# A two-layer decoder on one core: a third key block earlier, an output projection per tile, and copies moved to the head of a step

## The chip, the core and the metric

The kernel runs on one core of one Trainium2 chip. The metric is the time of one execution in device microseconds. TensorE does the matrix products (and transposes, as products with the identity), VectorE and ScalarE the elementwise work, GpSimd small operations and gathers, SyncE issues DMAs. The engines run their own instruction streams in program order and meet at semaphores.

## The reference

The input is eight sequences of 256 rows with 512 numbers each, and a context of the same shape. Two layers of three blocks each run over it, every block as a residual on a layer norm:

```
x = x + _L0_attn_ref(_layernorm(x, axis=-1), ...)     # 16 heads, rotary, causal window of 64
x = x + _L0_xattn_ref(_layernorm(x, axis=-1), ctx, mask, ...)   # 16 heads over the context
x = x + _L0_ffn_ref(_layernorm(x, axis=-1), ...)      # 64 experts, 6 per row, and a shared one
x = x + _L1_attn_ref(_layernorm(x, axis=-1), ...)     # state-space mixer in chunks
x = x + _L1_xattn_ref(_layernorm(x, axis=-1), ctx, ctx, gamma)  # 8 heads, attends over features
x = x + _L1_ffn_ref(_layernorm(x, axis=-1), ...)      # 8 low-rank experts on a dense layer
```

The change touches the parts that compute these lines. In the cross attention of layer 0 the context gives keys and values, and the result is divided by the sums of the exponentials:

```
k = _nan_clean(proj(at, Wk, bk, T))
probs = jax.nn.softmax(scores, axis=-1)
ctx = jnp.einsum('bhst,bhtd->bhsd', probs, v)
```

In layer 1 the mixer ends with `yn @ out_proj_w.T`, where yn are rows normalized per head; the attention after it computes `sm = softmax(q k * scale)` and `gamma * (sm v)` over 512 context features.

## The kernel before

The program has five stages, one after the other: phase 1 (both attentions of layer 0, function `phase1`), the shared expert with the router, the 64 experts, the mixers (function `mixers`, which holds the mixer and the attention of layer 1), and the feed-forward block of layer 1. In every stage each engine has its own function with an order written out by hand; `wait_ge` on a semaphore is the only thing that joins them. PSUM has eight banks, and `bank(n)` is one of them, 512 numbers on each of 128 partitions. Rows are handled in two tiles of 128 (NT = 2), the 512 columns in four blocks (KC = 4).

Phase 1 loops over the eight sequences. In the cross attention of sequence i the engines already begin with sequence i + 1: TensorE multiplies the keys of the next context, block by block (`keys`, through line 188), and ScalarE copies each block with its bias out of PSUM (`keys_copy`, line 615). Blocks 0 and 1 go to bank 7, blocks 2 and 3 to banks 2 and 3. At the end of the cross attention TensorE turns the next sequence's normalized rows (`rows_to_cols`, line 182), into banks 2 and 3 as well. VectorE takes the reciprocal of the sums of all heads (line 1102), TensorE spreads it over the 32 rows of each head with four products (line 934, into banks 0 and 1), ScalarE copies the two halves (line 710), VectorE multiplies them with the attention's result (line 1107), and TensorE applies the output projection (line 188 with `w_xo`). Between the spreads and the projection stand key blocks 2 and 3.

The mixers take the sequences in four pairs (`first`, `second`). At the end of a pair's mixer TensorE turns the gated rows of a sequence tile by tile (`turn_gated`, line 2404), ScalarE copies the two turned tiles (`gated_copy`, line 2212), and TensorE projects each tile (`project_out`, line 2473 through 188). The wait ahead of the projection of tile j asks for both copied tiles:

```
pe.wait_ge(sy["colsT_ready"], 8 * (s // 2) + 4 + NT * (b + 1))
```

Then comes the pair's attention, a loop of 32 steps (PAIRS = 16 for each sequence, HP = 32) with some steps behind. In step i TensorE makes the scores of two heads (line 2487), VectorE their minima (line 2756), ScalarE two exponentials (line 2310); two steps later TensorE turns the probabilities (line 2497), ScalarE and VectorE copy one half each (lines 2318 and 2763), and every second step TensorE multiplies them with the context (`returned`, line 2518). Each sequence has two groups of 16 heads. When a group's sums are complete, VectorE takes their reciprocals, TensorE turns them (`turn_recips`, line 2530, in steps 10, 17, 26 and 33), and ScalarE copies them to the tile `y` (`copy_recips`, line 2301, in steps 11, 18, 27 and 34). The turned reciprocals of group 0 lie in bank 7 and those of group 1 in bank 6; the products of the groups are collected in these banks too, so that `returned` waits for the copies before it begins a new group. In ScalarE's step the order was: exponentials of step i, turned copy of step i - 1, other work, copy of the reciprocals.

Of the kernel before, what the change touches and what calls it, by code (L numbers as in the profile page):

```python
# [40 lines left out]
NT = S // P  # L41
KC = D // P
# [291 lines left out]
def phase1(nc, sy, const, dr, held, nseq=NSEQ):  # L334
# [6 lines left out]
    with ExitStack() as ctx:  # L341
# [83 lines left out]
        def turned_in(i):  # L425
            return NT * 2 * i
# [2 lines left out]
            return NT * (2 * i + 1)  # L429

        def key_bank(i, c):
            return bank(7 if i >= 1 and c < 2 else 2 + c % 2)

        def turned_bank(at, j):
            return bank(2 + j if at and at % (2 * NT) == 0 else j)
# [157 lines left out]
        def _(act):  # L593
# [66 lines left out]
            for i in range(nseq):  # L660
                for c in range(2 * KC):
                    act.wait_ge(sy["qk_proj"], due("qk_proj", i, c + 1))
                    act.activation(qk_raw[:, c, :], bank(2 + c % 2)[:, 0:S], ACT.Copy,
                                   scale=-QK_SCALE if c < KC else 1.0).then_inc(sy["qk_raw_ready"], 1)
                    if i == 0:
                        split_hi(K if c < KC else V, c % KC)
                values_copy(i, 0)
                for n in range(LPAIRS):
                    c, r = n // 2, 2 * (n % 2)
                    act.wait_ge(sy["lmin_ready"], due("lmin_ready", i, n + 1))  # L670
                    if n >= 3:
                        act.wait_ge(sy["probsT_psum"], due("probsT_psum", i, n - 2))
                    for k in range(2):
                        scores = bank_pair(2 * (n % 2))[:, k, :]
                        act.activation(probs[:, n % 3, k, 0:P], scores[:, 0:P], ACT.Exp, bias=smin[:, n, k, 0:1],
                                       scale=-1.0, accum_out=ssum[:, c, 0, r + k:r + k + 1])
                        act.activation(probs[:, n % 3, k, P:S], scores[:, P:S], ACT.Exp,
                                       bias=smin[:, n, k, 1:2], scale=-1.0,
                                       accum_out=ssum[:, c, 1, r + k:r + k + 1]).then_inc(sy["probs_ready"], 1)
                    if n == 1:  # L680
                        values_copy(i, 1)
                    if i == 0 and 2 <= n < 2 + KC:
                        split_hi(XQ, n - 2)
                    if n in (5, 7):
                        copy_recips(i, (n - 5) // 2)
                copy_recips(i, 2)
                copy_recips(i, 3)
                if i == 0:
                    act.wait_ge(sy["w1b_in"], n_late * 16)
                    keys_copy(0, 0, KC)  # L690
                cols_copy(turned_attn(i))
                for c in range(KC):
                    act.wait_ge(sy["xq_psum"], due("xq_psum", i, c + 1))
                    act.activation(qk[:, c, :], bank(6 + c % 2)[:, 0:S], ACT.Identity, bias=bq[:, c:c + 1]
                                   ).then_inc(sy["xq_ready"], 1)
                for n in range(LPAIRS):
                    act.wait_ge(sy["clipped_ready"], due("clipped_ready", i, 2 * n + 2))
                    act.activation(xprobs[:, n % 4], xprobs[:, n % 4], ACT.Exp, scale=1.0 / ROOT_HD
                                   ).then_inc(sy["xprobs_ready"], 1)
                    if i < last and n in (0, LPAIRS - 1):  # L700
                        keys_copy(i + 1, n // (LPAIRS - 1), n // (LPAIRS - 1) + 1)
                    if i == last:
                        shared_opening(n)
                if i < last:
                    cols_copy(turned_in(i + 1))
                else:
                    shared_chunks_hi(2, 4)
                for half in range(2):
                    act.wait_ge(sy["xrecT_psum"], due("xrecT_psum", i, half + 1))
                    act.activation((cosq, sinq)[half][:].rearrange("p c s -> p (c s)"), bank(half)[:, :], ACT.Copy  # L710
                                   ).then_inc(sy["xrec_copied"], 1)
                if i < last:
                    keys_copy(i + 1, 2, KC)
                else:
                    shared_chunks_hi(4, len(MS_CHUNKS))
            sy.end_turn(act, 0, 0)
# [2 lines left out]
        def _(pe):  # L719
# [24 lines left out]
            def keys(i, chunks):  # L744

                for c in chunks:
                    if i == 0 and c >= 2:
                        pe.wait_ge(sy["xk_ready"], due("xk_ready", i, c - 1))
                    if i >= 1 and c == 1:
                        pe.wait_ge(sy["xk_ready"], due("xk_ready", i, 1))  # L750
                    if i >= 1 and c >= 2:
                        pe.wait_ge(sy["colsT_lo"], turned_in(i) + NT)
                    project_pe(pe, key_bank(i, c)[:, 0:S], lambda kc: w_x["k"][:, kc, c * P:(c + 1) * P],
                               lambda kc: ctxT[:, kc, :]).then_inc(sy["xk_psum"], 1)
# [118 lines left out]
            for i in range(nseq):  # L873
# [53 lines left out]
                pe.wait_ge(sy["clipped_ready"], due("clipped_ready", i, 2 * LPAIRS))  # L927
                if i < last:
                    rows_to_cols(hn, normed_in(i + 1), turned_in(i + 1))
                else:  # L930
                    shared_gate_up(0, 0)
                pe.wait_ge(sy["xrec_ready"], due("xrec_ready", i, 1))
# [3 lines left out]
                    if c % 2:  # L936
                        ins.then_inc(sy["xrecT_psum"], 1)
                if i < last:
                    keys(i + 1, range(2, KC))
                else:  # L940
                    shared_gate_up(0, 1)
                pe.wait_ge(sy["xattn_ready"], due("xattn_ready", i, 2))
# [1006 lines left out]
def mixers(nc, sy, const, dr, tiles, rows, router_raw, opening, nseq=NSEQ):  # L1949
# [3 lines left out]
    with ExitStack() as ctx:  # L1953
# [245 lines left out]
        def _(act):  # L2199
# [133 lines left out]
            for p in range(npair):  # L2333
# [33 lines left out]
                    high(first, j)  # L2367
                q0 = HP * p
                for i in range(HP + 3):
                    if i < HP:  # L2370
                        exponentials(q0 + i)
                    if p + 1 == npair and i == HP:
                        for j in range(NT):
                            ffn_rows_hi(j)
                    if 1 <= i <= HP:
                        turned_copy(q0 + i - 1)
                    if p + 1 == npair and i == 13:
                        ffn_fixed_hi()
                    if i in (8, 9):
                        high(second, i - 8)  # L2380
                    if i in (11, PAIRS + 11):
                        copy_recips(first + i // PAIRS, 0)
                    if i in (PAIRS + 2, HP + 2):
                        copy_recips(first + i // PAIRS - 1, 1)
                    if p + 1 < npair and i in (HP + 1, HP + 2):
                        rows_copy(first + 2 + i - HP - 1)
            act.wait_ge(sy["f_router"], 1)
# [4 lines left out]
        def _(pe):  # L2392
# [76 lines left out]

            def project_out(s, j):  # L2470
                b = s % 2
                pe.wait_ge(sy["colsT_ready"], 8 * (s // 2) + 4 + NT * (b + 1))
                project_pe(pe, bank(2 + 4 * b + j), lambda kc: hT[b][:, kc, j * P:(j + 1) * P],
                           lambda kc: w_mo[:, kc, :]).then_inc(sy["out_psum"], 1)

# [1025 lines left out]
```

## Time and profile before

| | us |
|---|---|
| median of 3 runs | 3139.12 (3132.17 to 3144.71) |
| profiled execution | 3157.93 |
| its span from first to last instruction | 3156.0 |
| TensorE busy | 2980.2 (94%) |
| VectorE busy | 2302.3 (73%) |
| ScalarE busy | 1579.9 (50%) |
| GpSimd busy | 809.4 (26%) |
| mean granted clock of TensorE | 0.98 |

The busy shares are means over stages with different limits; matrix products are pipelined and their ends are modelled. The granted clock is given as a share of full speed.

### The profile page before, as it was taken

What the parts mean: (1) busy time and instruction counts of PE and PEld (TensorE: products, weight loads), DVE (VectorE), ACT (ScalarE), POOL (GpSimd) and SP (SyncE); (2) the same over time, 40 slices, a digit from 0 to 9 for tenths busy, and PEclk for the clock granted to TensorE, in tenths of its full rate; (3) what the DMA queues carried; (4) which work ended last, traced back from release to release, by engine and by line L of the source; (5) the groups of instructions that cost most, each with busy time, mean ns of one, the idle gap of its engine ahead of it and who ended that gap; (6) DMA issues with size and microseconds to landing.
All of it is one profiled execution on the core that took longest, in us unless ns stands there. A gap on an engine that the chain in (4) does not pass through costs nothing. (4 is left out here: it accounts for less than half of the span.)

```text
span 3156.0 us, 61772 instructions
## 1 busy us (share of the span) xinstructions
PE 2980.2 (94%) x23073; PEld 2400.3 (76%) x23073; DVE 2302.3 (73%) x4321; ACT 1579.9 (50%) x3643; POOL 809.4 (26%) x974
## 2 busy tenths in 40 slices
PE   7999999998999999999999969999999989999999
PEld 5666666665998888888888846767666678888888
DVE  5665666665875788888888668878786877777776
ACT  3323333334221455555555436666666765555554
POOL 1221122121664111111111073341503022222222
PEclk9999999999999999999999979999999999999999
DMA  6325333321311677777777642121210042222222
GB/s 277 123 82 190 120 137 111 124 100 39 117 49 37 227 249 237 250 237 252 235 253 236 235 141 64 62 78 45 78 42 12 13 141 75 77 76 76 76 75 71
DMA packets 146539, 403.96 MB, mean 128 GB/s; under 512 B 39488, under 2 KB 48192, under 8 KB 133520
## 3 DMA queue, kind: packets, MB, share of 16 engines
q1 hardware_dynamic: 107888, 325.36, 30.0%
q0 software_dynamic: 18976, 50.45, 5.6%
q10 hardware_dynamic: 19456, 25.18, 2.3%
q8 instruction: 143, 2.34, 0.3%
q14 instruction: 76, 0.62, 0.1%
HBM read 344.06 MB, written 54.76 MB: 126 GB/s over the span
## 5 line engine op out<-in xcount | busy, mean ns | idle before, releaser
L288 POOL DMA_INDIRECT hr<-normed_rows,idx x128 | 123.3, 964 | 635.3 <-PE psum L302 592.6
L3016 POOL TENSOR_TENSOR mixf<-act 128x256 f32<-128x256 f32 x128 | 143.1, 1118 | 458.7 <-DVE act L3282 458.7
L174 POOL TENSOR_SCALAR ve<-mv 128x1 f32<-128x1 f32 x112 | 36.0, 321 | 791.4 <-DVE mv L965 523.0
L328 PE MATMUL psum<-xT_hi,wgu_hi 128*128 128x192 f32 (+1 forms) x1536 | 227.8, 270 | 1.4 <-PEq L1125 0.8
L328 PE MATMUL psum<-xT_hi,wgu_lo 128*128 128x192 f32 (+1 forms) x1536 | 223.1, 267 | 0.0
L328 PE MATMUL psum<-xT_lo,wgu_hi 128*128 128x192 f32 (+1 forms) x1536 | 222.6, 267 | 0.0
L1742 ACT ACTIVATE eth<-psum 128x192 f32<-128x192 f32 (+1 forms) x192 | 63.2, 330 | 299.1 <-PE psum L328 292.5
L328 PEld LDWEIGHTS psum<-xT_hi,wgu_hi 128*128 128x128 f32 (+1 forms) x1536 | 189.8, 182 | 26.6 <-ACT wgu_hi L1726 21.5
L2310 ACT ACTIVATE scratch<-psum,smin 128x512 f32<-128x512 f32 x256 | 173.7, 686 | 61.3 <-DVE smin L2756 59.1
L328 PEld LDWEIGHTS psum<-xT_hi,wgu_lo 128*128 128x128 f32 (+1 forms) x1536 | 190.3, 182 | 0.0
L328 PEld LDWEIGHTS psum<-xT_lo,wgu_hi 128*128 128x128 f32 (+1 forms) x1536 | 190.2, 182 | 0.0
L2756 DVE TENSOR_REDUCE smin<-psum 128x2 f32<-128x1024 f32 x128 | 155.4, 1217 | 37.2 <-PE psum L2487 36.5
L3282 DVE TENSOR_TENSOR act<-act,maskT 128x512 f32<-128x512 f32 x128 | 88.1, 689 | 116.9 <-ACT act L3058 116.4
L2497 PEld LDWEIGHTS psum<-ident,scratch 128*128 128x128 f32 x1024 | 110.6, 142 | 57.8 <-issue 38.9
L2497 PE MATMUL psum<-ident,scratch 128*128 128x128 f32 x1024 | 146.6, 283 | 6.1 <-DVE scratch L2763 2.9
L1852 DVE SCALAR_TENSOR_TENSOR eact<-eth,psum 128x192 f32<-128x192 f32 (+1 forms) x192 | 67.5, 352 | 111.9 <-ACT eth L1742 109.5
L3292 DVE TENSOR_TENSOR ca_lo<-act,ca_hi 128x512 fp32r<-128x512 f32 x128 | 134.2, 1049 | 12.4
L729 PE MATMUL psum<-hT_hi,w_slot 128*128 128x256 f32 x768 | 110.9, 289 | 11.9 <-ACT hT_hi L607 5.9
L1265 POOL DMA_INDIRECT slot_token<-tok_i,slot_w x96 | 104.6, 1090 | 67.5 <-DVE slot_r L1590 39.1
L2124 POOL DMA_INDIRECT yk<-expert_out,slots x84 | 86.1, 1025 | 122.9 <-issue 48.2
L1096 DVE TENSOR_SCALAR arena<-psum,hi 128x512 f32<-128x512 f32 x128 | 87.5, 745 | 40.7 <-PE psum L835 40.6
L3071 ACT ACTIVATE ca_hi<-act 128x512 fp32r<-128x512 f32 x128 | 81.0, 633 | 66.4 <-DVE act L3282 66.4
(466 smaller groups left out, 8681.9 us busy)
## 6 DMA issues: line engine op xcount, KB each, us to landing
w_sg<-in_w_gu_dram SPq DMA_DIRECT2D x32, 1408.0 KB
w_su<-in_w_gu_dram SPq DMA_DIRECT2D x32, 1408.0 KB
w_slot<-w_split SPq DMA_DIRECT2D x21, 2048.0 KB, 13.3
w_raw<-in_w_dram SPq DMA_DIRECT2D x128, 256.0 KB, 2.6
w_sd<-in_w_d_dram SPq DMA_DIRECT2D x32, 512.0 KB
wd<-in_w_d_dram SPq DMA_DIRECT2D x32, 512.0 KB
expert_out<-so ACTq DMA_DIRECT2D x64, 256.0 KB, 5.3
w_slot<-w_split SPq DMA_DIRECT2D x28, 512.0 KB, 5.1
```

The lines of the kernel that those rows point to most:

```text
L288: pool.indirect_dma_start(out=xg[0:w, t, :], out_offset=None, in_=rows, in_offset=bass.IndirectOffsetOnAxis(ap=idx[0:w, t:t + 1], axis=0)) ...
L328: ins = pe.matmul(bank(2 + m)[0:w, gu * CAP:(gu + 1) * CAP], wgu2[wp][:, gu, kc, m0:m0 + w], xT2[xp][:, kc, :], start=(i == 0 and kc == 0) ...
L729: ins = pe.matmul(out, lhs_of(lp, kc), rhs_of(rp, kc), start=(m == 0 and kc == 0), stop=(m == 2 and kc == KC - 1))
L1096: dve.tensor_scalar(xprobs[:, n % 4, kt], bank_pair(2 * (n % 2))[:, :, kt * S:(kt + 1) * S], hi[:, kt:kt + 1], -SCORE_CLIP * ROOT_HD, ALU. ...
L1265: pool.indirect_dma_start(out=dr["slot_token"], out_offset=bass.IndirectOffsetOnAxis(ap=slot_w[s % 2][:, j, k:k + 1], axis=0), in_=tok_i[s ...
L2124: pool.indirect_dma_start(out=gathered(s, NT * k + j), out_offset=None, in_=dr["expert_out"], in_offset=bass.IndirectOffsetOnAxis(ap=slots ...
L2310: act.activation(prob[:, q % 4, k, :], bank_pair(2 * (q % 2))[:, k, :], ACT.Exp, bias=smin[b][:, n, k:k + 1], scale=-1.0, accum_out=ssum[b ...
L2497: ins = pe.transpose(bank(4 + k)[:, mc * P:(mc + 1) * P], prob[:, q % 4, k, mc * P:(mc + 1) * P], ident)
L2756: dve.tensor_reduce(smin[(q // PAIRS) % 2][:, q % PAIRS, :], bank_pair(2 * (q % 2)), AX.X, ALU.min).then_inc(sy["smin_ready"], 1)
L3016: pool.tensor_tensor(mixf[:, g % LAG, :], act2[:, g % LAG, 0, :], act2[:, g % LAG, 1, :], ALU.add).then_inc(sy["f_mix"], 1)
L3282: dve.tensor_tensor(act2[:, g % LAG], act2[:, g % LAG], maskT[(g // FC) % 2][:, 2:4, :], ALU.mult).then_inc(sy["f_ca"], 1)
L3292: dve.tensor_tensor(ca2[1][:, g % LAG], act2[:, g % LAG], ca2[0][:, g % LAG].bitcast(F32), ALU.subtract).then_inc(sy["f_ca_lo"], 1)
```

## The change

In phase 1 key block 2 of the next sequence goes to bank 7, like blocks 0 and 1, and waits for the copy of block 1. TensorE multiplies it after the turned rows and ahead of the spreads; ScalarE copies it ahead of the two copies of the spread reciprocals. In the mixers the projection of tile j waits for the turned tiles up to j alone, and the copy of the turned reciprocals stands first in ScalarE's step.

```diff
         def key_bank(i, c):
-            return bank(7 if i >= 1 and c < 2 else 2 + c % 2)
+            return bank(7 if i >= 1 and c < 3 else 2 + c % 2)
...
                 if i < last:
                     cols_copy(turned_in(i + 1))
+                    keys_copy(i + 1, 2, 3)
                 else:
                     shared_chunks_hi(2, 4)
...
                 if i < last:
-                    keys_copy(i + 1, 2, KC)
+                    keys_copy(i + 1, 3, KC)
...
-                    if i >= 1 and c == 1:
-                        pe.wait_ge(sy["xk_ready"], due("xk_ready", i, 1))
-                    if i >= 1 and c >= 2:
+                    if i >= 1 and c in (1, 2):
+                        pe.wait_ge(sy["xk_ready"], due("xk_ready", i, c))
+                    if i >= 1 and c == 3:
                         pe.wait_ge(sy["colsT_lo"], turned_in(i) + NT)
...
                 if i < last:
                     rows_to_cols(hn, normed_in(i + 1), turned_in(i + 1))
+                    keys(i + 1, (2,))
...
                 if i < last:
-                    keys(i + 1, range(2, KC))
+                    keys(i + 1, (3,))
...
                 for i in range(HP + 3):
+                    if i in (11, PAIRS + 11):
+                        copy_recips(first + i // PAIRS, 0)
+                    if i in (PAIRS + 2, HP + 2):
+                        copy_recips(first + i // PAIRS - 1, 1)
                     if i < HP:
                         exponentials(q0 + i)
...
                     if i in (8, 9):
                         high(second, i - 8)
-                    if i in (11, PAIRS + 11):
-                        copy_recips(first + i // PAIRS, 0)
-                    if i in (PAIRS + 2, HP + 2):
-                        copy_recips(first + i // PAIRS - 1, 1)
...
             def project_out(s, j):
                 b = s % 2
-                pe.wait_ge(sy["colsT_ready"], 8 * (s // 2) + 4 + NT * (b + 1))
+                pe.wait_ge(sy["colsT_ready"], 8 * (s // 2) + 4 + NT * b + j + 1)
```

## Rows read from the trace of the kernel before

**Rows 1.** The page's first part: busy us (share of the span) xinstructions.

```profile
PE 2980.2 (94%) x23073; PEld 2400.3 (76%) x23073; DVE 2302.3 (73%) x4321; ACT 1579.9 (50%) x3643; POOL 809.4 (26%) x974
```

**Rows 2.** TensorE's waits, whole span: us in total, times, longest us.

```profile
PE psum L2518 <- ACT y L2301: 7.0, 6, 1.5
PE psum L188 <- ACT hT L2212: 6.8, 8, 1.1
...
PE psum L934 <- DVE recb L1102: 6.3, 8, 0.9
...
PE psum L2518 <- DVE scratch L2763: 3.2, 3, 1.4
```

**Rows 3.** Timeline, second transition: start, length, engine, line, operation [idle before <-releaser].

```profile
200.66 0.47 ACT L615 ACTIVATE xkT<-psum,bk 128x256 f32<-128x256 f32 x1 [0.99 <-PE psum L188]
...
202.55 1.76 DVE L1102 RECIPROCAL recb<-psum 128x256 f32<-128x256 f32 x1 [3.98 <-PE psum L853]
...
204.37 1.99 PE L934 MATMUL psum<-recb,spread 128*128 128x256 f32 x8 [0.86 <-DVE recb L1102]
205.53 0.60 ACT L710 ACTIVATE cosq<-psum 128x512 f32<-128x512 f32 x1 [1.34 <-PE psum L934]
...
206.20 3.62 PE L188 MATMUL psum<-ctxT,w_xk 128*128 128x256 f32 x16
...
207.03 0.69 DVE L1107 TENSOR_TENSOR oT<-psum,sinq 128x512 f32<-128x512 f32 x1 [0.17 <-ACT sinq L710]
...
209.65 7.03 PE L188 MATMUL psum<-w_xo,oT 128*128 128x512 f32 x16
```

**Rows 4.** Timeline around the second pair's projection of its second sequence.

```profile
2091.86 0.69 ACT L2290 ACTIVATE y<-y,grstd 128x128 f32<-128x128 f32 x2 [1.11 <-POOL grstd L2152]
...
2093.41 1.06 ACT L2212 ACTIVATE hT<-psum 128x512 f32<-128x512 f32 x2
...
2094.52 3.70 PE L188 MATMUL psum<-w_mo,hT 128*128 128x512 f32 x8 [1.11 <-ACT hT L2212]
...
2096.62 1.47 DVE L2750 SCALAR_TENSOR_TENSOR h_lo<-h,h_hi 128x512 fp32r<-128x512 f32 x2
```

**Rows 5.** Timeline, attention of the second pair, steps 10 to 13.

```profile
2124.25 0.66 PE L2530 MATMUL psum<-ident,y 128*128 128x128 f32 x4
...
2126.42 0.60 ACT L2318 ACTIVATE scratch<-psum 128x512 f32<-128x512 f32 x1 [0.35 <-PE psum L2497]
...
2128.91 0.69 ACT L2301 ACTIVATE y<-psum,small 128x512 f32<-128x512 f32 x1
...
2129.86 1.08 PE L2518 MATMUL psum<-scratch,cxT 128*32 128x128 f32 x32 [1.13 <-ACT y L2301]
...
2131.88 1.23 DVE L2756 TENSOR_REDUCE smin<-psum 128x2 f32<-128x1024 f32 x1 [1.65 <-PE psum L2487]
2132.46 0.60 ACT L2318 ACTIVATE scratch<-psum 128x512 f32<-128x512 f32 x1 [1.51 <-PE psum L2497]
```

**Rows 6.** Timeline, same attention, its second sequence, steps 27 to 29.

```profile
2172.39 0.69 ACT L2301 ACTIVATE y<-psum,small 128x512 f32<-128x512 f32 x1
...
2173.34 1.08 PE L2518 MATMUL psum<-scratch,cxT 128*32 128x128 f32 x32 [1.37 <-DVE scratch L2763]
...
2175.36 1.23 DVE L2756 TENSOR_REDUCE smin<-psum 128x2 f32<-128x1024 f32 x1 [1.22 <-PE psum L2487]
```

**Rows 7.** Two stretches between products: us, busy by engine, PEclk, DMA, GB/s.

```profile
2001.84:2010.65 8.81, 8.81 (x60) 6.27 (x60) 5.95 (x11) 3.98 (x10) 1.15 (x4) 0.50 0.01 2
2173.34:2178.18 4.84, 4.84 (x60) 3.49 (x60) 3.55 (x6) 3.24 (x10) 0.79 (x2) 1.00 0.00 0
```

**Rows 8.** Stretches from spread to spread in phase 1, and their sum.

```profile
204.37:295.34 90.97, 86.13 (x713) 58.92 (x713) 57.66 (x100) 32.58 (x100) 18.09 (x25) 1.00 0.46 173
...
572.76:670.20 97.44, 91.90 (x712) 62.71 (x712) 57.96 (x100) 32.79 (x100) 18.10 (x25) 0.93 0.31 111
...
sum 651.12, PE 613.68 PEld 419.11 DVE 402.72 ACT 232.70 POOL 127.00; mean PE 87.67 PEld 59.87 DVE 57.53 ACT 33.24 POOL 18.14
```

## The prediction

> **What bounds the kernel now.** I read the page's busy shares first: TensorE is busy for 94% of the span [rows 1], so the time is the length of its instruction stream plus its waits. The second view is the list of TensorE's waits. Three of its lines stand on places that the change touches [rows 2]: the spread matmuls wait for the reciprocal on VectorE (6.3 us in 8 waits), the mixers' output projection for the turned rows that ScalarE copies (6.8 us in 8), and the products of the second attention (L2518) for the copied reciprocals (7.0 us in 6). A fourth line, L2518 on VectorE's copy, 3.2 us in 3, belongs to the third partly; I come back to it. The third view is the timeline around one case of each, to see whether the other engines stand still at the same time. Only if they do is a removed wait given back as time.
>
> **Part one, key block 2 ahead of the spreads (seven transitions between sequences).** Before, TensorE turns the next rows, waits 0.86 us for the 1.76 us reciprocal, runs the eight spread records, then sixteen records of key blocks 2 and 3, and then the output projection [rows 3]. The waits add to 6.3 over eight; the last sequence has no next keys and is not changed, and seven times 0.86 is 6.0. Nothing is added or removed: eight matmul records, and on ScalarE one copy of 0.47 us, come earlier. From start to start the sixteen records take 209.65 - 206.20 = 3.45 us, so one block is 1.73. It fits into the wait and sticks out by 1.73 - 0.86 = 0.87 at most, so that the spreads run 0.8 to 0.9 later than now, counted from the turned rows.
>
> What is late next is the chain spread, ScalarE copy, VectorE product, for which the projection waits. Now the second product ends at 207.03 + 0.69 = 207.72 and the projection starts at 209.65, 1.93 later, covered by both key blocks [rows 3]. Afterwards the chain ends 0.8 to 0.9 later (208.5 to 208.6) while the projection wants to start 0.86 earlier (208.8). About 0.2 us of cover is left. The moved ScalarE copy (0.47) has its block ready when the spreads start, and the first spread copy comes 1.16 after their start, behind 1.34 of ScalarE idle; the moved copy lies in that. The new wait of block 2, for the copy of block 1 in the same bank, is long met: that kind of copy ends at 200.66 + 0.47 = 201.13, over 2 us before the turned rows are done at 204.37 - 0.86 = 203.51. Behind the waiting block would stand the spreads and all that follows. Bounds per transition: 0.86 gained, or, if the cover of 0.2 is overrun by the whole moved copy, 0.86 - 0.5. I take 0.86, seven times: **6.0 us**. No DMA moves; those of SyncE that follow (weights of the next sequence) wait for TensorE's own products and move along.
>
> The ends of TensorE's rows deserve care. By starts alone, the projection would move up by the spreads' first record too, a little more than the gap. The Trainium skill (Perfetto Trace Analysis, section Tensor Engine Instruction) says that TensorE's end times are computed and not observed; a sum from starts would be up to about 0.94 per transition, 6.6 us in place of 6.0. The trace agrees that ends overlap: the spreads' row ends at 204.37 + 1.99 = 206.36 and the next begins at 206.20 [rows 3].
>
> **Part two, the output projection per turned tile (four pairs of sequences).** The eight waits are of two kinds: four of 1.1 (second sequence of a pair), which leaves 6.8 - 4.4 = 2.4, or 0.6 each, for the first. In the second, ScalarE copies two tiles in 1.06 from 2093.41, and TensorE starts 0.05 after the second, with 1.11 of waiting [rows 4]. With a wait per tile it starts after the first: 1.06 / 2 = 0.5 earlier. The scores behind it need the low part of the normalized rows, whose first tile is there by about 2096.62 + 0.73 = 2097.4, while the projection, 3.70 long, ends near 2097.7 even then. So 0.5 is kept; four pairs give **2.0 us**. In the first sequence the same 0.5 is gained at the projection but not kept: the next thing on TensorE is the turning of the second sequence, which needs ScalarE's scaled rows, done at 2091.86 + 0.69 = 2092.55 after a wait for GpSimd [rows 4], and that chain is not driven by TensorE. The copies at 2093.41 follow from there as now, so I take 0. Bounds for the part: 0 and 6.8.
>
> **Part three, the copies of the turned reciprocals at the head of ScalarE's step.** Sixteen copies, of which four (the last of each pair) come in a step that has nothing ahead of them; twelve move in front of two exponentials and a turned copy. Of these the eight with group 0 hold TensorE up. In one loop [rows 5]: the reciprocals are turned by 2124.25 + 0.66 = 2124.91. ScalarE reaches the head of the step at 2126.42 + 0.60 = 2127.02 but copies only at 2128.91, and L2518 starts at 2129.86 after 1.13 of waiting. From 2127.02 the copy would be done at 2127.7, before TensorE gets there at 2128.73: the wait goes whole. Do the others follow? The next minima on VectorE had stood idle for 1.65 and ScalarE's next turned copy for 1.51, both behind TensorE [rows 5]; both hold more than 1.13. The price on ScalarE is that two exponentials come up to 0.69 later, the copy's length, but the exponentials after them come at the same time as now, since the copy has only changed places, and the 1.51 of idle lie right behind. What is next in line afterwards is VectorE with 0.5 to spare.
>
> In the second sequence of two pairs the same wait is put down to VectorE's copy, 1.37 [rows 6]. There L2518 starts 0.26 after the end of the ScalarE copy (2172.39 + 0.69 = 2173.08), exactly as in rows 5 (2129.60 to 2129.86). It is the same wait, named wrongly. VectorE's idle time behind it is 1.22, so 1.22 is what can be gained. The sum: 7.0 for the six and 2 x 1.22 = 2.4, **9.4 us**. The four copies of group 1 in the eighteenth step delay nobody that I can see, and I count them as 0; their bounds are 4 x 0.69 = 2.8 lost and, should a loop wait unseen, as much gained.
>
> Here a rule speaks against the change. The row shows ScalarE with the copy behind work that was ready later. The Trainium skill (TensorE: Matmul & The Clock Gate, section Architectural detail: the array is 16× 32×32, not 1× 128×128) says that ScalarE works its queue strictly in order; so a copy at the head whose reciprocals are not yet turned holds all exponentials of the step. By the rule alone each lateness would be paid in full; by the rows the reciprocals are ready 2.1 us ahead of the head (2124.91 to 2127.02), and it costs nothing. The trace agrees with the order that the rule states.
>
> **The clock.** In the first pair's second sequence TensorE fell to half of its 2.4 GHz right at the 1.5 us wait for the copy; the stretch between two products took 8.81 at 0.50 against 4.84 at 1.00 in the next pair [rows 7]. If the fall goes with its wait, 4.0 more are won. I count half, 2.0, since falls also come where no wait of this size goes.
>
> **The sum.** 6.0 + 2.0 + 9.4 + 2.0 = 19.4 us. The profiled execution took 3157.9, so 3138.5 for its like. The runs shown have a median of 3139.1, 18.8 below it, and I take that distance as unchanged: **3119.7, rounded 3120 us**.
>
> **Rivals.**
> - The cover at the projection of phase 1 is overrun. For it: 0.2 us is little, and the moved copy of 0.47 stands ahead of the spread copies. Against: ScalarE idles there. It takes 0.5 x 7 = 3.5 back: 3123.2.
> - ScalarE becomes the end of the attention loop: twelve late pairs of exponentials cost 12 x 0.69 = 8.3. For it: in the steps before, ScalarE runs nearly without gaps. Against: its 1.51 idle behind each copy [rows 5]. 3128.0.
> - The copy does not release the product: L2518 waits in truth for the turned probabilities that ScalarE copies just ahead of the reciprocals. Then 9.4 stay: 3129.1. Against it speaks the program: that product needs turned copies only up to the one of 2126.42.
> - Slower: the clock. In phase 1 a sequence takes 90.97 at a granted clock of 1.00 and 97.44 at 0.93; the seven together take 651.1 [rows 8], 14.3 above seven of the fast ones. A shorter sequence meets the clock's decisions in another phase. If all seven ran as the slow one, they would take 682.1, 31.0 more; less the gain of the other terms (17.4) that is 13.6 slower: 3152.7. It decides from 17.4 / 6.5, some three further sequences. For it: the falls differ between sequences of the same work. Against: the change takes idle time out of TensorE and puts none in.
>
> **Chances.** Forecast 0.66, the cover 0.10, ScalarE 0.11, the product's other wait 0.07, the clock 0.06. What a measurement can tell from no change is about 0.5%, 15.7 us: faster means below 3123.4, slower above 3154.8. The forecast is over the bound with 0.55 of its 0.66 (without the clock's 2.0 it stands at 3121.7, only 1.7 below the bound), the first rival with half; together 0.60 faster. Half of the clock's case goes beyond the bound upward, 0.03. The rest, 0.37, is the same. The range: at the low end the whole of the 4.0 and half of the 14.3 go with the waits, 3119.7 - 2.0 - 7.2 = 3110; at the high end it takes in the second and third rival, 3131. The forecast's own range is 3113 to 3125.
>
> **What would show it.** Right: no wait before the spreads but key records there; about 90.1 between the spreads of two sequences at clock 1.00; the wait at L188 for the copied tile down to 0.5 in the second sequences and near 0 in the first; L2518 without a wait on the copied reciprocals in all eight loops, and VectorE's idle of 1.65 down to about 0.5. Wrong: a new wait of the projection on VectorE's product in phase 1; exponentials that make the scores or the turning wait; more stretches at half clock.

## Result and profile after

The changed kernel takes 3114.27 us in the median of 5 runs (3109.52 to 3115.61), the kernel before 3138.83 in the median of 5 beside them: ratio 0.9921, interval [0.9907, 0.9934], 24.6 us faster. Set against the kernel before once more on another chip (run e9_whole below) it took 3113.98 against 3134.10: ratio 0.9931 [0.9916, 0.9946], 20.1 us. The forecast was 3120, in a range of 3110 to 3131. The profiled execution after took 3110.33, its span is 3108.5, its mean granted clock 0.988 (before: span 3156.0, clock 0.980). Of the runs below one, of e1_keys, took 9496.98 us, three times the others, and is left out of that kernel's median.

The two profiled executions differ by 47.6 us, nearly twice what the medians differ by, so they can't be subtracted as wholes. Most of the surplus lies ahead of the mixers. Their first projection starts at 1912.35 in the profile before, but at 1894.85 and 1895.60 in two experiments that leave all work ahead of it as before (e2_project, e3_copies). About 17 us belong to that one execution, near the 18.8 by which it lies over the median. Below, stretches are compared place by place.

The page's line of busy times after, which answers to [rows 1]; TensorE's busy time counts its slow stretches at their length:

```profile
PE 2954.8 (95%) x23073; PEld 2384.2 (77%) x23073; DVE 2301.0 (74%) x4321; ACT 1579.0 (51%) x3643; POOL 808.7 (26%) x974
```

The counts are the same; VectorE, ScalarE and GpSimd are busy as long as before, within 1.3 us. TensorE's waits after (us in total, times, longest), the lines that answer to [rows 2]:

```profile
PE psum L2489 <- ACT scratch L2312: 2.8, 9, 0.3
...
PE psum L188 <- ACT hT L2214: 2.5, 4, 0.6
...
PE psum L2406 <- ACT y L2292: 1.3, 4, 0.5
...
PE psum L2520 <- DVE scratch L2765: 0.4, 1, 0.4
PE psum L936 <- DVE recb L1104: 0.3, 1, 0.3
```

The spreads now wait in the last sequence alone, which has no next keys. The projection's wait is down from 6.8 in 8 to 2.5 in 4. The product (L2518 before, L2520 now) has no line on the copied reciprocals any more, and the one on VectorE's copy fell from 3.2 to 0.4. Some waits have grown a little: the scores wait 2.8 us in 9 for exponentials (L2489; before, as L2487, 2.5 in 8), and the turning of the gated rows waits 1.3 in 4 for ScalarE's scaled rows (L2406; before, as L2404, 0.4 in 1). The timeline of the second transition, beside [rows 3]; its first row is of the kernel before, the others are of the kernel after:

```profile
202.42 1.09 PE L182 MATMUL psum<-ident,hn 128*128 128x128 f32 x8
```

```profile
201.90 1.09 PE L182 MATMUL psum<-ident,hn 128*128 128x128 f32 x8
202.03 1.76 DVE L1104 RECIPROCAL recb<-psum 128x256 f32<-128x256 f32 x1 [3.98 <-PE psum L854]
...
202.82 1.89 PE L188 MATMUL psum<-ctxT,w_xk 128*128 128x256 f32 x8
...
204.55 1.89 PE L936 MATMUL psum<-recb,spread 128*128 128x256 f32 x8
204.75 0.47 ACT L615 ACTIVATE xkT<-psum,bk 128x256 f32<-128x256 f32 x1 [1.08 <-PE psum L188]
205.62 0.60 ACT L711 ACTIVATE cosq<-psum 128x512 f32<-128x512 f32 x1 [0.39 <-PE psum L936]
...
206.28 1.89 PE L188 MATMUL psum<-ctxT,w_xk 128*128 128x256 f32 x8
...
207.11 0.69 DVE L1109 TENSOR_TENSOR oT<-psum,sinq 128x512 f32<-128x512 f32 x1 [0.17 <-ACT sinq L711]
...
208.01 3.17 PE L188 MATMUL psum<-w_xo,oT 128*128 128x512 f32 x7
```

The reciprocal ends at 203.79, under the key block, and the spreads start without a wait. From the start of the turned rows to that of the projection it is 208.01 - 201.90 = 6.11; before, it was 209.65 - 202.42 = 7.23. The second product ends at 207.80, 0.21 ahead of the projection: that is all the cover that is left.

The second pair's projection of its second sequence, beside [rows 4], waits 0.63 in place of 1.11 and starts behind the first of the two tiles of the copy at 2056.19. What it gains the scores keep, for the low part follows 2.09 after its start, as before (2.10):

```profile
2054.64 0.70 ACT L2292 ACTIVATE y<-y,grstd 128x128 f32<-128x128 f32 x2 [1.11 <-POOL grstd L2154]
...
2056.19 1.06 ACT L2214 ACTIVATE hT<-psum 128x512 f32<-128x512 f32 x2
...
2056.82 3.70 PE L188 MATMUL psum<-w_mo,hT 128*128 128x512 f32 x8 [0.63 <-ACT hT L2214]
...
2058.91 1.47 DVE L2752 SCALAR_TENSOR_TENSOR h_lo<-h,h_hi 128x512 fp32r<-128x512 f32 x2
```

The same pair's attention, steps 10 to 13 of the first sequence and 27 to 28 of the second, beside [rows 5, 6]:

```profile
2086.56 0.66 PE L2532 MATMUL psum<-ident,y 128*128 128x128 f32 x4
...
2088.73 0.60 ACT L2320 ACTIVATE scratch<-psum 128x512 f32<-128x512 f32 x1 [0.36 <-PE psum L2499]
...
2089.22 0.68 ACT L2303 ACTIVATE y<-psum,small 128x512 f32<-128x512 f32 x1
...
2090.98 1.08 PE L2520 MATMUL psum<-scratch,cxT 128*32 128x128 f32 x32
...
2093.00 1.23 DVE L2758 TENSOR_REDUCE smin<-psum 128x2 f32<-128x1024 f32 x1 [0.45 <-PE psum L2489]
2093.58 0.60 ACT L2320 ACTIVATE scratch<-psum 128x512 f32<-128x512 f32 x1 [0.51 <-PE psum L2499]
...
2131.31 0.69 ACT L2303 ACTIVATE y<-psum,small 128x512 f32<-128x512 f32 x1
...
2133.01 1.08 PE L2520 MATMUL psum<-scratch,cxT 128*32 128x128 f32 x32
```

The reciprocals are turned by 2087.22, the head of the step comes at 2089.22, the copy is done at 2089.90, and the product starts 1.08 later without a wait. VectorE's idle time behind it fell from 1.65 to 0.45, ScalarE's from 1.51 to 0.51. Counted from the pair's first projection, in us of the profiled executions (a product is counted at its start, the last one at the start of its last record):

| place | before | after |
|---|---|---|
| product of step 12, pairs 2 and 3 | 44.49, 44.50 | 43.32, 43.32 |
| product of step 28, pairs 2 and 3 | 87.97, 87.97 | 85.35, 85.33 |
| last product, pairs 2, 3 and 4 | 102.64, 102.64, 101.09 | 100.12, 100.12, 98.62 |

Two windows of after from the product of step 28 to the next (us, busy by engine, granted clock, DMA share, GB/s), in the first and the second pair, beside [rows 7]: the first pair's is at full clock now, 5.37 in place of 8.81.

```profile
1969.88:1975.25 5.37, 5.14 (x62) 3.54 (x61) 5.30 (x10) 3.86 (x11) 0.79 (x2) 1.00 0.00 2
2133.01:2137.84 4.83, 4.83 (x62) 3.48 (x61) 4.76 (x8) 4.32 (x13) 0.79 (x2) 1.00 0.01 2
```

And the second and the last stretch from spread to spread, beside [rows 8]: the second is 1.14 shorter than before at the same clock of 1.00, and stretches are still longer where the clock falls.

```profile
204.55:294.38 89.83, 85.88 (x713) 59.00 (x712) 57.63 (x100) 32.58 (x100) 18.03 (x25) 1.00 0.47 175
655.18:748.03 92.85, 85.71 (x702) 57.21 (x700) 55.69 (x96) 36.81 (x108) 18.72 (x23) 0.96 0.19 66
```

### The profile page after: what moved, and what is told of

The parts are those of the page before. It is cut to its first block and busy times, and to the rows that moved or that the text cites. A ratio compares the mean times of both kernels' runs of the same rounds, so it can differ in the third digit from the quotient of the medians.

```text
span 3108.5 us, 61772 instructions
## 1 busy us (share of the span) xinstructions
PE 2954.8 (95%) x23073; PEld 2384.2 (77%) x23073; DVE 2301.0 (74%) x4321; ACT 1579.0 (51%) x3643; POOL 808.7 (26%) x974
```

## Experiments

The theory is that of the prediction: three separate waits, each given back as time. The first four kernels take the change apart; the next four put a strain on what the theory says is hidden. "Before" is the median of the kernel before on the same chip: 3137.45 for the first four, 3135.17 for the next four, 3134.10 for the last two.

**e1_keys: the key block alone.** The whole change without its two edits in the mixers:

```diff
-   pe.wait_ge(sy["colsT_ready"], 8 * (s // 2) + 4 + NT * b + j + 1)
+   pe.wait_ge(sy["colsT_ready"], 8 * (s // 2) + 4 + NT * (b + 1))
...   (both groups' copy_recips back behind high(second, i - 8))
```

> The key block alone: key block 2 ahead of the spreads, everything else as before. Theory (the removed waits are worth their start-to-start length): from spread to spread 89.8 us at full clock in place of 90.97, that is 1.13 us in each of seven transitions, 7.9 us together, so about 3131 against 3138.8; the mixers' waits stay (L188 on the copied tile 1.1 us, L2518 on the copied reciprocals 1.1 us). Rival A (the gap of 0.86 in the profile is the whole gain): 90.1 and 6.0 us. Rival B (the gain of the whole change came from the clock): a time anywhere in 3130 to 3140 with 89.8, and fewer stretches at half clock.

Measured: 3128.2 in the median of six runs, 9.3 under the kernel before, ratio 0.9965 [0.9953, 0.9977]. From spread to spread, here the second stretch:

```profile
204.19:294.03 89.84, 85.86 (x714) 58.84 (x713) 57.64 (x100) 32.61 (x100) 18.09 (x25) 1.00 0.47 175
```

That is 90.97 - 89.84 = 1.13 per transition, and seven of them 7.9 us. So rival A is out: the gap of 0.86 in [rows 3] was too small a measure.

**e2_project: the projection per turned tile alone.**

```diff
-   pe.wait_ge(sy["colsT_ready"], 8 * (s // 2) + 4 + NT * (b + 1))
+   pe.wait_ge(sy["colsT_ready"], 8 * (s // 2) + 4 + NT * b + j + 1)
```

> The output projection per turned tile alone. Theory: in each of four pairs TensorE's wait for the second copied tile goes (0.6 us in the first sequence, about 0.5 of 1.1 in the second); in the first it is taken back by the turning of the second sequence, so 0.5 us a pair are kept, 2 us together: 3136 to 3137 against 3138.8. Rival (both are kept): 1.0 us a pair, 4 us, 3134 to 3135.

Measured: 3135.34, 2.1 under, ratio 0.9994 [0.9983, 1.0006]. The interval holds 1, so the time alone shows nothing. The profile does: the wait is 2.5 in 4, as in the whole change, the turning of the gated rows waits 1.3 in 4 in place of 0.4 in 1, which is where the first sequences' gain goes, and from the second pair's first projection to the third's it is 166.54, against 167.00 in e1_keys, whose mixers are those of before. That is 0.46 per pair, and four pairs give 1.8.

**e3_copies: the copies at the head alone.**

```diff
     for i in range(HP + 3):
+        if i in (11, PAIRS + 11):
+            copy_recips(first + i // PAIRS, 0)
+        if i in (PAIRS + 2, HP + 2):
+            copy_recips(first + i // PAIRS - 1, 1)
         if i < HP:
             exponentials(q0 + i)
...
         if i in (8, 9):
             high(second, i - 8)
-        if i in (11, PAIRS + 11):
...
```

> The copies of the turned reciprocals at the head of ScalarE's step alone (both groups). Theory: all eight waits of L2518 for the copied reciprocals go and the pair's attention is 2.4 to 2.7 us shorter, 10.4 us together without the clock; 3126 to 3129. Rival (ScalarE becomes the end of the loop): the waits go but the attention is less than 1 us shorter in each pair, 3135 to 3139.

Measured: 3126.81, 10.6 under, ratio 0.9965 [0.9948, 0.9983]. The last products of pairs 2 to 4 come at 100.12, 100.13 and 98.61 from the first projection, as in the whole change; from pair to pair it is 164.50 against 167.00. ScalarE does not become the end of the loop. In its list of waits the product's line has gone, those of the other two parts have stayed:

```profile
PE psum L188 <- ACT hT L2212: 6.8, 8, 1.1
PE psum L934 <- DVE recb L1102: 6.3, 8, 0.9
...
PE psum L2518 <- DVE scratch L2763: 0.4, 1, 0.4
```

The line on VectorE's copy (3.2 before) went to 0.4 by moving a ScalarE copy alone: it was the same wait, put down to the other engine.

**e4_group0: the whole change, with group 1's copies at their old place.**

```diff
     for i in range(HP + 3):
         if i in (11, PAIRS + 11):
             copy_recips(first + i // PAIRS, 0)
-        if i in (PAIRS + 2, HP + 2):
-            copy_recips(first + i // PAIRS - 1, 1)
...
+        if i in (PAIRS + 2, HP + 2):
+            copy_recips(first + i // PAIRS - 1, 1)
         if p + 1 < npair and i in (HP + 1, HP + 2):
```

> The whole change, but with the copy of group 1 (steps 18 and 34) at its old place in ScalarE's step. Theory (the copies of group 1 delay nobody): the same as the whole change within 1 us, 3113 to 3116, and the attention of a pair as long as there within 0.2 us. Rival (they cost or give up to their length, 0.69 in each of four loops): 2.8 us more or less than the whole change, and the stretch from the product of step 12 to that of step 20 longer or shorter by 0.5 to 0.7.

Measured: 3112.89, ratio 0.9917 [0.9899, 0.9934], and in the third pair the last product at 100.13, as with group 1 moved (100.12). Group 1's move is worth nothing that the runs show, either way.

**e5_both_blocks: key block 3 ahead of the spreads as well.** This takes away the last cover of the chain spread, ScalarE, VectorE.

```diff
-   return bank(7 if i >= 1 and c < 3 else 2 + c % 2)
+   return bank(7 if i >= 1 else 2 + c % 2)
...
-   keys(i + 1, (2,))
+   keys(i + 1, (2, 3))
...   (block 3 waits for block 2's copy; its own copy goes ahead of the spread copies)
```

> The whole change, and key block 3 ahead of the spreads too (in bank 7, behind the copy of block 2). Theory (what is left between spreads and projection must cover the chain spread, ScalarE copy, VectorE product, and only 0.2 us of cover is left in the whole change): the spreads come 1.7 us plus a wait of 0.6 to 0.8 for the bank later, and the projection then waits about 1.5 to 1.9 us for VectorE's second product, so a transition is 2.1 to 2.4 us longer than in the whole change, 15 to 17 us together: 3129 to 3131. Rival (the chain is no bound, TensorE's stream alone is): 0.6 to 0.8 us a transition for the bank's wait, 5 us: 3119.

Measured: 3129.81, ratio 0.9985 [0.9976, 0.9995], 15.5 above the whole change by medians of two chips. Spread to spread takes 92.37, 2.54 more than after. This agrees with the theory and not with the rival. The first line is from the list of waits, the others from the timeline of the second transition:

```profile
PE psum L188 <- DVE oT L1103: 9.9, 7, 1.4
```

```profile
204.89 1.89 PE L188 MATMUL psum<-ctxT,w_xk 128*128 128x256 f32 x8
207.35 1.99 PE L188 MATMUL psum<-ctxT,w_xk 128*128 128x256 f32 x8 [0.56 <-ACT xkT L615]
209.18 1.89 PE L932 MATMUL psum<-recb,spread 128*128 128x256 f32 x8
...
211.74 0.69 DVE L1103 TENSOR_TENSOR oT<-psum,sinq 128x512 f32<-128x512 f32 x1 [0.17 <-ACT sinq L711]
212.48 2.84 PE L188 MATMUL psum<-w_xo,oT 128*128 128x512 f32 x6 [1.41 <-DVE oT L1103]
```

The projection waits 1.41 in all seven transitions, until 0.05 after the second product ends (212.43). Block 3 waits besides for the copy of block 2 in the one bank, 0.56 here. Counted from start to start, against 1.73 for such a row without a wait, the two are 212.48 - 209.18 - 1.73 = 1.57 and 207.35 - 204.89 - 1.73 = 0.73, and block 3's own row, behind the wait, takes 0.10 more: 2.40 of the 2.54. So a block behind the spreads is needed, and with one the cover just suffices.

**e6_context_later: the whole change, and the copy of the second sequence's turned context behind that of its gated rows.** It aims at the 0.6 that is left of the projection's wait.

```diff
-    context_high(second)
     gated_copy(second)
+    context_high(second)
```

> The whole change, and ScalarE's copy of the next context's high part (1.04 us) behind the copies of the second sequence's turned rows instead of ahead of them. Theory (in the second sequence ScalarE's context copy, not TensorE, holds the turned rows up): the wait at L188 in the second sequences goes from 0.6 to 0.5 or less and the copies start 0.4 to 0.5 us earlier, worth 0.4 us in each of four pairs, 1.6 us: 3112 to 3113. Rival (the low parts of the normalized rows are late next): 0, and the scores behind the projection wait for VectorE.

Measured: 3112.32, ratio 0.9927 [0.9910, 0.9944]. The projection's waits are down to 1.0 in 4. The second sequence's projection starts 8.77 after the first's in place of 9.16, and the 0.39 is kept to the last product (99.72 against 100.12, counted from the first projection in the second pair).

**e7_between: the copies between exponentials and turned copy.**

```diff
     for i in range(HP + 3):
+        if i < HP:
+            exponentials(q0 + i)
         if i in (11, PAIRS + 11):
...
-        if i < HP:
-            exponentials(q0 + i)
```

> The whole change, but with the copies of the turned reciprocals between the step's exponentials and its turned copy. Theory (the product L2518 is released by this copy alone): the copy ends 0.6 us earlier than before the change and 1.4 later than at the head, so L2518 waits 0.4 to 0.7 us in all eight loops and the time is 3 to 5 us above the whole change, 3117 to 3120. Rival 1 (the turned copy releases it): L2518 waits 1.1 or more again, 3123 or more. Rival 2 (ScalarE is the end of the loop): no wait, and the time of the whole change.

Measured: 3121.90, ratio 0.9948 [0.9931, 0.9966], 7.6 above the whole change and above the range of the theory. The six runs go from 3109.80 to 3123.37: two, with a mean clock of 0.988 and 0.989, lie at 3114.97 and 3109.80, as low as the whole change, and four, with 0.985, at 3121.47 or more. So the time alone separates the two kernels poorly, and the profile has to. The waits have one line again; then the second pair's timeline at step 11, and the window of the first pair's step 28:

```profile
PE psum L2520 <- ACT y L2303: 5.8, 8, 1.0
```

```profile
2096.52 0.69 ACT L2303 ACTIVATE y<-psum,small 128x512 f32<-128x512 f32 x1
...
2097.45 1.08 PE L2520 MATMUL psum<-scratch,cxT 128*32 128x128 f32 x32 [0.63 <-ACT y L2303]
```

```profile
1971.61:1980.42 8.81, 8.81 (x61) 6.27 (x61) 6.44 (x11) 4.21 (x11) 1.15 (x4) 0.50 0.01 2
```

The product starts 0.24 after the copy's end (0.26 in [rows 5]), and step 12's comes 0.72 later than in the whole change, 0.45 earlier than before. The last products are 1.59, 1.55 and 1.37 later in pairs 2 to 4. It is the two exponentials ahead of the copy that cost, more than the turned copy: 0.72 of the 1.17 that the whole move gains at step 12. The first pair has its half-clock stretch again, 8.81 at 0.50, as before; the theory had left that out.

**e8_step_earlier: group 0's copies at the head of the step before.** Here the copy meets reciprocals that aren't turned yet.

```diff
-        if i in (11, PAIRS + 11):
+        if i in (10, PAIRS + 10):
             copy_recips(first + i // PAIRS, 0)
```

> The whole change, but with the copies of group 0 at the head of the step before (10 and 26), ahead of the turning of the reciprocals on TensorE. Theory (ScalarE takes its queue in order, and the margin of about 2 us at the head of step 11 is what makes the copy free): the copy waits 0.5 to 1 us at the head of step 10 for TensorE's turned reciprocals and the exponentials of step 10 start about 1.1 us later; the loop has some 0.4 us of slack there, so 0.3 to 0.8 us are lost in each of eight loops, 3117 to 3121. Rival (the wait is hidden, since the exponentials wait for VectorE's minima anyway): the time of the whole change.

Measured: 3115.33, ratio 0.9941 [0.9923, 0.9959], below the theory's range and within 1.4 of both medians of the whole change, so the time alone shows no loss. The second pair's timeline, step 10 of its first sequence:

```profile
2090.27 0.65 PE L2532 MATMUL psum<-ident,y 128*128 128x128 f32 x4
...
2090.96 0.69 ACT L2303 ACTIVATE y<-psum,small 128x512 f32<-128x512 f32 x1 [0.49 <-PE psum L2532]
...
2091.55 0.68 ACT L2312 ACTIVATE scratch<-psum,smin 128x512 f32<-128x512 f32 x1
...
2093.13 0.49 PE L2489 MATMUL psum<-cx_hi,h_hi 32*128 32x512 f32 x2 [0.28 <-ACT scratch L2312]
```

ScalarE waits 0.49 at the copy with the exponentials behind it, and TensorE's scores then wait 0.28 for the exponentials. The rule that spoke against the change, ScalarE's strict order in the Trainium skill (TensorE: Matmul & The Clock Gate, section Architectural detail: the array is 16× 32×32, not 1× 128×128), agrees with the row. Step 12's product comes 0.33 later than in the whole change, the last of the pair 0.57; over the four pairs it is 2.2, the low end of what was expected. So the place has a floor: one step earlier the copy pays for its order in the queue, and at the head of step 11 it doesn't.

**e9_whole and e10_later_again: the whole change and e6_context_later side by side.** The edits are those shown.

> The whole change, unaltered, once more on the chip of the next run, for a direct comparison with it. Theory (the parts add): 3112 to 3117 us. If the earlier 24.6 us held several us of luck with the clock, it comes nearer to the sum of the parts alone, 20.9 us under the kernel before.

> The whole change with the copy of the turned context of the second sequence behind that of its gated rows. Theory: the 0.39 us that the profile showed in each of four pairs is kept, so 1.6 us under the whole change in the run beside it. Rival: it is given back later in the pair, and the two are equal within 0.5 us.

Measured: 3113.98, ratio 0.9931 [0.9916, 0.9946], and 3112.23, ratio 0.9928 [0.9913, 0.9943]. The second is 1.75 under the first by medians, but their runs overlap (3110.61 to 3115.41, 3108.41 to 3114.57). By the profile the later context copy brings the second projection 0.38 to 0.39 forward in pairs 2 to 4, in both of its executions, and 0.37 to 0.41 of it is there at the product after step 28's. It has the lowest median of the kernels, by a difference that the profile shows and the times alone can't.

## Why the prediction was right

**The key block: right in kind, its size too small (6.0 forecast, 7.9 measured).** The step that failed is "the waits add to 6.3 over eight ... seven times 0.86". From start to start the transition was 1.95 (turned rows to spreads), 1.83 (spreads), 3.45 (two blocks), 7.23 in all. Now it is 0.92 (turned rows), 1.73 (block 2), 1.73 (spreads) and 1.73 (block 3), 6.11. So the wait was 1.95 - 0.92 = 1.03 by starts, for the row ahead of it is drawn with an end that reaches into the gap: that row is 1.09 long, yet the next starts 0.92 after it where nothing waits. The Trainium skill (Perfetto Trace Analysis, section Tensor Engine Instruction) says that such ends are computed, and the two rows agree. Another 0.10 is the spreads' slower first record, which went with the wait. The estimate from starts in the prediction (0.94, which no row shows) pointed the right way and was passed over; it still lacked most of the overlap. The cover at the projection is the forecast 0.2 (0.21) by luck, for its terms were off and cancel: the spreads run 0.70 later and not 0.87 (2.65 after the turned rows in place of 1.95), the chain behind them is 0.10 shorter, and the projection comes 1.12 earlier and not 0.86. The first rival did not come; e5_both_blocks shows that it looked at the right place, for there the projection waits once its cover is gone.

**The projection: right (2.0 forecast).** The second sequences' waits fell from 1.1 to 0.6, and the first sequences' 0.6 went from the list. The pair got 0.46 shorter, once, not twice (e2_project), as the chain over GpSimd in [rows 4] said: the first sequence's gain stands as a wait at the next turning (L2406, 1.3 in 4). The time of that part alone lies within what can be told from no change.

**The copies: right, a little small (9.4 forecast, 10.3 measured).** Pairs 2 to 4 end 2.52, 2.52 and 2.47 earlier; in the first pair the product of step 12 comes 1.17 earlier from the scores, and step 28's 1.62 earlier from the eighth, 2.79 together. The step that was small is the 1.22 for the second sequences of pairs 2 and 3, which was VectorE's idle time: TensorE's own wait was 1.37 [rows 6], and from the product of step 20 to that of step 28 it gained 22.63 - 21.19 = 1.44, of which the last steps give back 0.1. The rest is again that a printed wait is a little too small: 1.13 in step 12 of the second pair gave 1.17, and the fourth pair's waits of 1.11 and 1.12 gave 2.47. The third rival, that the product waits for the turned probabilities, is wrong: with the copy ahead of them the wait is gone (e3_copies), with it between exponentials and probabilities over half of it stays (e7_between, 5.8 in 8). The second, that ScalarE becomes the end, is wrong: its idle time of 1.51 took up the late exponentials, and 0.51 is left. The sign of it that the prediction named, exponentials that make the scores wait, is there only in small: the scores wait 2.8 us in place of 2.5, and the turning of the probabilities 6.9 in place of 5.4 for the two copies of turned halves (3.9 and 3.0, before 2.9 and 2.5); some 0.1 of the gain is gone by the pair's last product.

**The clock at the first pair: right at its place, the gain not shown (2.0 of 4.0 forecast).** The stretch at step 28 is 8.81 at half clock in the kernel before, in e1_keys and in e7_between and 8.38 (at 0.53) in e2_project, the four profiles in which the product waits there. It is 5.37 in all eight profiles without the wait. So 3.4 was to be had at this place, not 4.0: the first pair needs 5.37 at full clock where the second needs 4.84. But mostly the half clock only moves. The stretch from that product to the next pair's first projection, in e1_keys, in the profile after and in e9_whole, the same kernel once more:

```profile
1975.06:2057.16 82.10, 79.20 (x515) 62.60 (x515) 61.63 (x134) 47.54 (x130) 43.62 (x58) 0.92 0.26 78
```

```profile
1969.88:2047.66 77.78, 74.10 (x515) 58.51 (x515) 61.86 (x134) 47.55 (x132) 43.71 (x58) 1.00 0.28 83
```

```profile
1967.56:2049.75 82.19, 78.41 (x515) 62.44 (x514) 60.94 (x134) 47.52 (x132) 43.63 (x58) 0.94 0.26 78
```

With the wait the four profiles take 80.32 to 83.53. Without it three (after, e5_both_blocks, e10_later_again) take 77.75 to 77.81 at a clock of 1.00, and five (e3_copies, e4_group0, e6_context_later, e8_step_earlier, e9_whole) 81.08 to 82.21 at 0.94 to 0.96, as long as with it (0.5 of such a difference is the projection's, where a kernel has that edit). So the step "If the fall goes with its wait, 4.0 more are won" failed: the fall left its place in eight of eight, and the time was won in three of eight. On the mean the eight are 1.6 shorter than the four, less than the scatter within either group, so the 2.0 of the sum is neither shown nor refuted.

**The clock in phase 1.** The slower rival, more falls in phase 1, did not come; there were fewer. The seven stretches from spread to spread take 647.78 to 651.12 in the three profiles with the old phase 1 (before, e2_project, e3_copies) and 633.30 to 636.54 in the eight with one key block moved. The nearest two are e3_copies and e1_keys:

```profile
sum 647.78, PE 610.82 PEld 416.97 DVE 402.51 ACT 232.81 POOL 127.28; mean PE 87.26 PEld 59.57 DVE 57.50 ACT 33.26 POOL 18.18
```

```profile
sum 636.54, PE 605.46 PEld 413.68 DVE 401.58 ACT 232.81 POOL 127.27; mean PE 86.49 PEld 59.10 DVE 57.37 ACT 33.26 POOL 18.18
```

They differ by 11.2, more than the 7.9 of the keys. Of the seven stretches five or six lie below a clock of 1.00 in the three profiles, and two to four in the eight. So with the moved block falls are rarer here, in eight profiles against three, which the prediction's sum had at nothing and only the low end of its range allowed for. What of it stays to the end is open: e1_keys is 9.3 faster by its runs, and their mean clock over the whole execution (0.983 to 0.985) is that of the kernel before (0.980 to 0.986).

**The sum.** By places it is 7.9 + 1.8 + 10.3 = 20.0, and the clock comes on top in some executions. The parts alone, by medians, give 9.3 + 2.1 + 10.6 = 22.0 (the expectation of e9_whole has 20.9, with another median of e1_keys, over all its seven runs). The whole gave 24.6 beside one set of runs and 20.1 beside another; its own two medians, 3114.27 and 3113.98, agree, and those of the kernel before differ by 4.7. The parts add within that spread. The forecast of 3119.7 was 5.4 too high: 1.9 at the keys and 0.9 at the copies, less 0.2 at the projection, make 2.6, and the rest is within the spread of the runs and the clock. Taking the profiled execution's distance from the median as unchanged did no harm, for it lay ahead of the mixers, in that execution alone.

## What to carry to other kernels

A wait on a saturated TensorE is measured from start to start of the rows around it, with the same rows without the wait as the yardstick; the gap that the profile prints was 0.86 where 1.13 was to be had. Work moved into such a wait needs a count of what stays behind it: one key block left 0.21 of cover, and moving the second cost 2.5 per transition. A copy in an engine's ordered queue has a best place, between the moment its input is ready and the first work that can wait: behind the two exponentials it left waits of 0.5 to 1.0, a step earlier it cost 0.3, and at the head of the right step nothing. A fall of the clock that went with a wait left its place when the wait was removed, but in five of eight profiles the time was lost again behind it: what such a fall is worth is counted to an event well behind, over more than one execution.

## Not expected of the hardware

One wait of 1.0 to 1.5 us of TensorE in the first pair goes with a fall of the granted clock to 0.50 (0.53 over the place in e2_project), the lower of its two levels (1.2 GHz), in four profiles of four, and the eight profiles without the wait have 1.00 there, though five of them have their half clock further on, around the pair's last product or behind it. The waits of like length in the second pair are at full clock in the same profiles [rows 7], though e1_keys has such a stretch in its third pair too (8.82); what tells them apart was not tried.

In the profile before, the first two steps from a pair's last product to the next pair's first projection take 65.62 and 65.59, where e1_keys, with the same mixers, needs 64.38 for each. Some 1.2 of it lies with a wait of VectorE for a TensorE product there (2.30 and 2.28 in place of 1.05). No other profile shows this in the first two steps, and its cause is open. In the third step every profile has that wait at 2.37 to 2.38, e1_keys too, without being longer for it.
